# An attention kernel with six local-attention layers: v_back's large transfers in the next step, and a loop over batches written out

## The reference

```python
def attn_layer(x, Wqkv, qs, ksc, Wo):          # 16 heads of 64, windows of 32 tokens
    q, k, v = split_heads(x @ Wqkv)
    q, k = rotary(l2norm(q) * qs), rotary(l2norm(k) * ksc)
    return local_attention(q, k, v) @ Wo       # each window sees itself and the window before it
for i in range(6):
    x = attn_layer(shift_tokens(x), ...) + x
    x = ffn_layer(shift_tokens(x), ...) + x    # layernorm, W1, a * gelu(gate), W2
```

## Time and profile before

| what | value |
|---|---|
| median of 3 runs | 4634.17 us (4632.89 to 4639.07) |
| profiled execution | 4644.36 us, span 4642.6 us |
| busy share of the span | PE 89%, PEld 60%, DVE 62%, ACT 56%, POOL 58% |
| granted TensorE clock, mean | 0.950 |
| first attention | about the first 911 us |
| local layers | from about 916 us on |

### The profile page before, as it was taken

The page is one execution under the profiler, slowest core; times in us unless marked ns, Lnnn a source line. Parts: engine busy times, 40 slices in busy tenths (PEclk is TensorE's granted clock), DMA queues, the critical chain, the costliest instruction groups (busy, mean ns, idle before and its releaser), DMA issues. The chain is left out here.

```text
span 4642.6 us, 152879 instructions
## 1 busy us (share of the span) xinstructions
PE 4130.6 (89%) x66876; PEld 2769.5 (60%) x66876; DVE 2893.4 (62%) x4211; ACT 2615.3 (56%) x4412; POOL 2707.4 (58%) x3440
## 2 busy tenths in 40 slices
PE   5879788679999999999999999999999999999994
PEld 2434344346666666666666666666666666666663
DVE  5565656456666666666666656666666666666664
ACT  2545353445555556666666655555656556666662
POOL 0000000067777777778777867677767777777781
PEclk9989898889999999999999999999999999999997
DMA  0000000111111211112211212111221112221122
GB/s 28 3 16 2 15 2 16 38 42 46 44 47 46 67 51 46 47 46 71 58 49 48 57 51 56 45 46 46 61 55 46 46 46 55 57 62 50 47 59 79
DMA packets 246285, 208.29 MB, mean 45 GB/s; under 512 B 118461, under 2 KB 227224, under 8 KB 235256
## 3 DMA queue, kind: packets, MB, share of 16 engines
q1 hardware_dynamic: 245624, 198.51, 16.3%
HBM read 68.01 MB, written 29.77 MB: 21 GB/s over the span
## 5 line engine op out<-in xcount | busy, mean ns | idle before, releaser
L782 DVE TENSOR_TENSOR products<-bank_d,table 128x1024 f32<-128x1024 f32 x768 | 933.1, 1215 | 861.8 <-ACT sq L609 840.9
L905 POOL TENSOR_TENSOR products<-products 128x2048 f32<-128x2048 f32 x192 | 871.8, 4541 | 458.4 <-DVE products L782 458.4
L410 PE MATMUL bank_d<-w_qkv,xT 128*128 128x512 f32 x1536 | 830.8, 656 | 14.4 <-issue 5.8
L609 ACT ACTIVATE sq<-bank_d 128x512 f32<-128x512 f32 x768 | 465.5, 606 | 449.9 <-PE bank_d L410 437.8
L942 POOL TENSOR_TENSOR qk_rot<-products,rnorm 128x2048 f32<-128x2048 f32 x192 | 695.7, 3624 | 7.6
L780 DVE TENSOR_REDUCE ss<-sq 128x16 f32<-128x1024 f32 x384 | 465.6, 1213 | 123.3 <-ACT sq L609 123.0
L869 POOL MEMSET ident<- 128x128 f32 x1 | 0.2, 205 | 911.0 <-POOLq L1060 911.0
L949 POOL TENSOR_TENSOR prob<-prob,inv_sum 128x1024 f32<-128x1024 f32 x192 | 365.4, 1903 | 250.7 <-DVE inv_sum L762 250.7
L1487 DVE TENSOR_REDUCE part_max<-s_max 128x1 f32<-128x512 f32 (+3 forms) x768 | 398.6, 554 | 150.7 <-PE s_max L1236 101.9
L440 PE MATMUL bank_a<-probT,v 64*64 64x32 f32 x12288 | 397.1, 222 | 60.4 <-issue 60.4
L656 ACT ACTIVATE attnT<-bank_a 128x512 f32<-128x512 f32 x384 | 208.4, 594 | 428.1 <-PE bank_a L440 428.1
(11 more groups left out here) (166 smaller groups left out, 7220.4 us busy)
## 6 DMA issues: line engine op xcount, KB each, us to landing
v_back<-v SPq DMA_DIRECT2D x96, 768.0 KB, 5.4
v_back<-v SPq DMA_DIRECT2D x192, 128.0 KB, 5.4
xs<-x_layers SPq DMA_DIRECT2D x194, 64.0 KB, 2.1
xr<-x_layers SPq DMA_DIRECT2D x96, 128.0 KB, 2.7
x<-x SPq DMA_DIRECT2D x96, 128.0 KB, 1.8
xs<-x SPq DMA_DIRECT2D x192, 64.0 KB
x_layers<-x SPq DMA_DIRECT2D x96, 128.0 KB, 1.8
w_qkv<-in_Wqkv_dram SPq DMA_DIRECT2D x7, 1024.0 KB, 5.1
```

The source lines that it names most:

```text
L410: nc.tensor.matmul(bank[:, :], xT[:, P * a:P * (a + 1)], w_qkv[:, col:col + 512], start=True, stop=True).then_inc(d_filled if i < 8 else a ...
L609: nc.scalar.activation(sq[j % 2][:, 8 * c:8 * c + 8, :], bank_d[slot][:, :].rearrange("p (h d) -> p h d", d=DH), ACT.Square).then_inc(squa ...
L782: nc.vector.tensor_tensor(products[:, a, head:head + 8, :, :].rearrange("p h r (o d) -> p h r o d", o=2), bank[:, :].rearrange("p (h r d) ...
L905: link(nc.gpsimd.tensor_tensor(products[:, a, :, 0, :], products[:, a, :, 0, :], products[:, a, :, 1, :], ALU.add))
```

## The change

The two transfers of v_back that read only the pair's own values (768 KB and 128 KB) are taken out of the pair's own step. They are issued in the next step, after SyncE has seen that both halves of that step's scores are done (`scores_ready`). The third, of 128 KB, stays and gets semaphores of its own, `v_last_in`. TensorE now waits for both before `times_v`; ScalarE waits only for the small one before it overwrites `v`. In the first attention, the loop over batches 1 to 3 is written out, so that all wait values are constants.

```diff
@@ -333,6 +334,12 @@
                     load_w_qkv((s.layer + 1) % DEPTH, 0, 2 * INNER, wqk_in)
+                if runs(back1):
+
+                    sp.wait_ge(scores_ready, 2 * back1.n + 2)
+                    src, dst, done = v[back1.par], v_back[back1.par], v_back_in[back1.par]
+                    sp.dma_start(dst[WINDOW:P, :, :], src[0:P - WINDOW, :, :]).then_inc(done, 16)
+                    sp.dma_start(dst[0:WINDOW, 1, :], src[P - WINDOW:P, 0, :]).then_inc(done, 16)
                 if runs(back2):
@@ -352,12 +359,8 @@
                     sp.wait_ge(a_free, ring_a.at(s, (1, "v", 1))[1] + 1)
-                    q = WINDOW
-                    src, old, dst = v[now.par], v[1 - now.par], v_back[now.par]
-                    done = v_back_in[now.par]
-                    sp.dma_start(dst[q:P, :, :], src[0:P - q, :, :]).then_inc(done, 16)
-                    sp.dma_start(dst[0:q, 1, :], src[P - q:P, 0, :]).then_inc(done, 16)
-                    sp.dma_start(dst[0:q, 0, :], old[P - q:P, 1, :]).then_inc(done, 16)
+                    sp.dma_start(v_back[now.par][0:WINDOW, 0, :], v[1 - now.par][P - WINDOW:P, 1, :]).then_inc(
+                        v_last_in[now.par], 16)
@@ -426,7 +429,8 @@
                 if half == 0:
-                    pe.wait_ge(v_back_in[pair.par], 48 * (pair.k + 1))
+                    pe.wait_ge(v_last_in[pair.par], 16 * (pair.k + 1))
+                    pe.wait_ge(v_back_in[pair.par], 32 * (pair.k + 1))
@@ -617,7 +621,7 @@
-                    act.wait_ge(v_back_in[1 - now.par], 48 * (prev(s).pair(0).k + 1))
+                    act.wait_ge(v_last_in[1 - now.par], 16 * (prev(s).pair(0).k + 1))
@@ -1132,8 +1136,7 @@
         def batches(eng, body):
-            body(0)
-            with nc.Fori(1, BATCH, engines=[eng.engine], hint_back_edge=True) as b:
+            for b in range(BATCH):
                 body(b)
```

More of the change, by code:

```diff
@@ L218, in local_layers @@
         v_back_in = [sem(f"v_back_in{i}") for i in range(2)]
+        v_last_in = [sem(f"v_last_in{i}") for i in range(2)]
         x1_out, x2_out = sem("x1_out"), sem("x2_out")
```

## The result

The changed kernel took 4468.83 us (median of 4 runs, 4462.97 to 4471.0), the kernel before 4633.64 us (4 runs, 4632.89 to 4639.07). The ratio is 0.964, 95% interval 0.9623 to 0.9657: 165 us less. The forecast was 4468. Its profiled execution took 4468.73 us, with a span of 4467.0; that of before took 4644.36, so between the two traces, which are what follows compares, the difference is 175.6 us.

What follows compares the result with a forecast made beforehand. TensorE bounds each step, and in long steps waits for instruction fetches held behind v_back's transfers. Of 216 us, 161 saved plus 3 for the loop took 4644.36 to 4480; less 10.2 for the median, 4470, stated as 4468, range 4410 to 4540.

Steps and rivals of the forecast that it cites:

- The moved transfers are hidden: After the scores: transfers issued 13.4 us before times_v, landing in 5.4 to 6 us; a fetch late there costs nothing.
- own stalls in times_v: Where a page ends as times_v starts, TensorE outruns its fetch: 15 to 19 steps of 1.5 us, 28 us stay.
- the 128 KB and weights at the change of layers: Beside times_v, the remaining small transfer and, at five layer ends, line 277's weights: 8 us stay, bounds 0 and 58.
- scores: TensorE's own stalls in the scores, 1.50 us at 2612.48: partly in the 35.43 already, 6 us added.
- the base: Step length of 35.43 us, mean of the 18-step middle stretch, against which long steps were priced at 216 us.
- The waits for "issue" under 50 us: Sign that the forecast is right: line 444's waits for "issue" fall from 156.9 us to under 50.
- The loop, 3 us: First attention: writing out the loop saves about 1 us per batch, 3 us for three batches, bounds 0 to 8.
- The last step of the sum: From profiled execution to median: 4480 less the 10.2 us by which the runs' median lay lower, 4470, given as 4468.
- Rival 1: Beside times_v, the remaining small transfer still delays the fetch by 0.9 us: 78 us more, 4545 us; chance 0.12.
- Rival 2: Stalls come from the pace of times_v alone, so moving v_back gains nothing: 4631 us; chance 0.04.
- Rival 3: Large transfers land late and times_v waits for them; at a landing of 17 us, 4812 us; chance 0.04.
- The cycle of 64 steps: The extra wait makes a step 1,276 instructions, 4 short of five pages, so the stall pattern repeats every 64 steps.

Runs made afterwards that it cites:

- e4: Kernel before, transfers in their old place, met waits added so a page ends 155 instructions into times_v in every step: 4775.9 us, ratio 1.0306.
- e3: Kernel before, transfers in their old place, met waits added so a page ends 55 instructions into times_v, first three steps unaligned: 4444.01 us, ratio 0.9587.
- e8: Changed kernel with met waits added so a page ends 155 instructions into times_v in every step: 4440.38 us, ratio 0.9579.
- e7: Changed kernel with the two moved transfers issued only for the first two pairs, later pairs using stale values: 4463.73 us, ratio 0.9645.
- e6: Changed kernel with the last 128 KB transfer of v_back moved too, for all steps but the first: 4469.87 us, ratio 0.9647.
- e9: Changed kernel with met waits added so a page ends 240 instructions into times_v in every step: 4640.9 us, ratio 1.003.
- e5: Changed kernel with met waits added so a page ends 50 instructions into times_v in every step: 4410.17 us, ratio 0.9517.
- e2: Kernel before with only the loop over batches written out, v_back's transfers as before: 4637.83 us, ratio 1.0006.
- e10: Kernel before with only the transfers moved and the loop kept, run again on another chip beside the changed kernel: 4468.94 us, ratio 0.9658.
- e1: Kernel before with only the transfers moved and the loop over batches kept, first run: 4488.77 us, ratio 0.9684.
- e12: Kernel before, transfers in their old place, met waits added so a page ends 50 instructions into times_v from the first step on: 4436.76 us, ratio 0.9569.

## Why the prediction was right, and where its terms were off

**What bounds the kernel: right.** That TensorE waits for its program behind v_back's transfers, only where the page's end falls badly, was inferred from one fetch in one long step and a count. e4 against e3 (332 us by the place alone), e4 against e8 (335 us by the transfers alone, at one place), and the fetch that moves 5.3 us into times_v in e4 and 1.9 in e8 show it.

**The moved transfers are hidden: right.** 13.3 us between issue and times_v, 5.2 us to land, as forecast; e7 shows that their presence there costs nothing measurable.

**The sum: right in total, with terms that cancelled.** The steps before had 236 us above 35.20 each; the forecast took away 161 and so left 75. Adding up the changed kernel's steps above 35.20 (by line 341; shorter ones left out) leaves 60:

| what stays | forecast, us | measured, us |
|---|---|---|
| own stalls in times_v (steps 19 to 28, 78 to 93) | 28 | 36 |
| the 128 KB and weights at the change of layers (steps 15, 16, 64, 80) | 8 | 7 |
| scores (steps 48 to 62) | 26, of which 20 in the base of 35.43 | 12 |
| first steps | 8 | 4 |
| second wait | 5 | 0 |

The split of the first two rows is by the steps' position; e6 shows that the 128 KB have no part. The weights of line 277, which the prediction priced, leave steps 14, 30 and 46 at 35.2 us. Steps 16, 64 and 80 hold the load of w_o in a layer's second step, which the prediction did not name, and step 15 holds neither. So this term came out at its size for another reason. The term most off is the base: I took 35.43, the mean of a stretch that itself held score stalls, for a clear step of 35.20, and so left such stalls in all 64 long steps, 20 us, where the changed kernel has 12 in all. The term for own stalls was too small: I looked for them where the page ends as times_v starts, 15 to 19 steps, and put later stalls down to the transfers; 9 steps of the first pass and 13 of the second have them, with ends, by my count, from about 205 to 250, and e9 prices the place at 2.5 us a step instead of 1.5.

**The waits for "issue" under 50 us: missed.** They are 67.1. For the same reason: own stalls are more than I thought. Even e5, with all ends in a clear place, has 35.2 us of them, about 0.35 each, which are the ordinary gaps ahead of times_v. The bound of 50 left only 15 for real stalls.

**The loop, 3 us: wrong in size, it gives 0.** The 0.7 us of one stretch are little more than the 0.5 us by which the same code differs between two runs (batch 0, before and e2), and the layers start no earlier: line 362's first start is 946.5, line 358's was 945.0, and e2 and e10 show no gain. A difference inside one batch was carried to the whole without asking how much such a stretch scatters.

**The last step of the sum** took the 10.2 us by which the profiled execution of before lay above its median off again. In the traces the gain was 175.6, not 164; between the medians it was 165. The exact hit at 4468 is thus partly luck: the sum was 12 us short, and the changed kernel's profiled execution did not lie above its median.

**The rivals.** Rival 1 (the small transfer holds the fetch) falls with e6 and e8. Rival 2 (pace of times_v alone) falls with e3 and e4 as the cause of what the change gained, but names rightly what it left, as e9 shows. Rival 3 (transfers late) falls with the landing of 5.2 us. The rule of the Trainium skill (Runtime: NRT & Kernel Launch, section Instruction fetch mechanics) that the crossing is mostly hidden falls with e4 and e9. The cycle of 64 steps holds roughly: the groups of long steps in times_v end at steps 28 and 93, 65 apart.

**Still open:** why e1 was 20 us slower on its chip; what stalls e12's scores in the second steps of the layers; and whether moving the w_o load would take e8's last 14 us.

## What to carry to other kernels

When TensorE stops for "issue" in a dense run of small matmuls, take the length of every step, not the mean, count instructions per step modulo the 256 of a fetched page, and look whether a large transfer is issued just ahead of the missing fetch. Then move the transfer to a sparse stretch, and also place the pages' ends: some ever-met waits that bring a step to whole pages were worth 200 us on the kernel before and 58 on the changed one. And test such a change at two places of the page's end, since any edit of TensorE's instruction count shifts it: the same edit was worth 24, 165 or 335 us.

## What was not expected of the hardware

- The place of the page ends in TensorE's program decides 332 us of 4444 (e3, e4), with the work of a step equal.
- Without any large transfer near, an end at 240 costs 2.5 us per step (e9), although the stall in the first half is 1.40 us in the step shown. Part of the rest falls at the clock of 0.50 behind it: in the changed kernel four matmuls of line 413 take 3.59 us behind such a stall (at 4130.64), and 1.98 in a clear step (at 2486.83).
- From the packet of an instruction fetch to TensorE's going on it is 2.7 to 2.8 us in three runs (changed kernel, e4, e9), which is longer than 256 of its instructions last in times_v.
- Two waits on semaphores went into one instruction: ten per step shifted the page's end by the five that made it stand still, and q8 counts 3 fetches more than before in e3 (536 against 533), where the 1,070 added waits would fill 4 pages of 256 at one instruction each.
